# Expert biases spread by TensorE, gate columns stored apart, one expert's weights moved behind a store

## The reference, cut to what matters

```python
y = depthwise_causal_conv(x, cond)                 # called z in the kernel
logits = einsum('bsd,de->bse', y, Wr)
w, sel = top_k(logits, 2); w = softmax(w)
gate = einsum('bsk,bske->bse', w, one_hot(sel))
for e in range(8):
    out = out + gate[..., e:e+1] * (einsum('bsd,df->bsf', y, We[e]) + be[e])
return x + out
```

## Time and profile before

| | us |
|---|---|
| median of 3 runs (lowest, highest) | 823.74 (822.41, 827.26) |
| the profiled execution | 826.98 |
| its span in the profile | 824.9 |
| TensorE busy | 725.0 |
| VectorE, ScalarE, GpSimd busy | 532.0, 437.5, 503.9 |
| mean granted TensorE clock, share of full speed | 0.952 |

### The profile page before, as it was taken

How to read it: one execution, slowest core, us unless ns; L and a number is a source line. 1 busy time by engine, 2 the same in 40 slices (tenths; PEclk the granted TensorE clock), 3 DMA queues, 4 the chain that set the end, 5 groups by cost and what they waited for, 6 DMA issues and landing times.

```text
span 824.9 us, 13278 instructions
## 1 busy us (share of the span) xinstructions
PE 725.0 (88%) x3769; PEld 477.0 (58%) x3808; DVE 532.0 (64%) x765; ACT 437.5 (53%) x721; POOL 503.9 (61%) x760
## 2 busy tenths in 40 slices
PE   1753689999999999999999969995679999999995
PEld 0111235555555555565555559994558888888883
DVE  2466989898889888848876533576454445454542
ACT  2054457777778777847777511573443333434331
POOL 1036788787777777748773420003568888888773
PEclk9985889999999999989999988998799999999998
DMA  9986135566776766646667557698978989888983
GB/s 357 387 312 182 33 64 100 122 131 150 146 166 138 142 147 150 136 102 137 135 123 133 105 100 163 130 301 208 277 159 156 161 162 160 164 157 164 159 156 41
DMA packets 233113, 132.25 MB, mean 160 GB/s; under 512 B 182402, under 2 KB 198786, under 8 KB 231890
## 3 DMA queue, kind: packets, MB, share of 16 engines
q1 hardware_dynamic: 212866, 93.75, 46.8%
q0 software_dynamic: 15904, 35.48, 23.3%
q10 hardware_dynamic: 4272, 2.18, 1.3%
HBM read 74.44 MB, written 37.78 MB: 136 GB/s over the span
## 4 chain that ended last, share of the span: by engine, by line
PE 74%; DMA 10%; SPq 7%; DVE 3%; issue 2%; POOL 2%; ACT 1%; POOLq 0%; DVEq 0%; ACTq 0%
PE PS L1758 21%; PE PS L1615 12%; PE PS L1592 12%; PE PS L1604 12%; PE PS L1669 7%; PE PS L1636 3%; PE PS L1740 3%; DMA WRAW<-in_We 3%; SPq L429 3%; DMA WRT<-in_Wr 2%; PE PS L1645 2%; DMA z_scratch<-ZS 2%; PE PS L1627 2%; DMA QyT<-Qy 2%; SPq L515 1%
## 5 line engine op out<-in xcount | busy, mean ns | idle before, releaser
L1758 PE MATMUL PS<-W,ZH 128*128 x568 | 184.7, 406 | 7.1 <-DVE ZL L1498 7.0
L1592 PE MATMUL PS<-W,QyT 128*128 128x512 bf16 x499 | 126.0, 393 | 28.2 <-DMA QyT<-Qy 17.8
L869 POOL DMA_INDIRECT ZR<-z_scratch,IDG x71 | 78.9, 1112 | 94.6 <-DVE IDG L1466 60.6
L878 POOL DMA_INDIRECT out_x<-YS,IDS x71 | 112.7, 1587 | 39.3 <-issue 19.5
L1104 ACT ACTIVATE YS<-YS,SG 128x512 f32<-128x512 f32 x71 | 51.4, 724 | 138.5 <-DVE YS L1517 130.9
L1604 PE MATMUL PS<-W,QyT 128*128 128x512 bf16 x500 | 122.4, 384 | 0.6
L1758 PEld LDWEIGHTS PS<-W,ZH 128*128 128x128 f32 x568 | 103.1, 191 | 26.8 <-issue 8.4
L1615 PE MATMUL PS<-W,QT 128*128 128x512 bf16 x498 | 113.8, 379 | 0.7
L1498 DVE TENSOR_TENSOR ZL<-PS,ZH 128x512 fp32r<-128x512 f32 x71 | 49.1, 692 | 100.0 <-ACT ZH L1093 100.0
L1758 PE MATMUL PS<-W,ZL 128*128 x284 | 112.5, 396 | 0.0
L939 ACT ACTIVATE SG<-PS,sm 128x1024 f32<-128x1024 f32 x64 | 71.4, 1115 | 60.2 <-PE PS L1592 60.2
(11 more groups left out here) (249 smaller groups left out, 1110.9 us busy)
## 6 DMA issues: line engine op xcount, KB each, us to landing
X<-in_x SPq DMA_DIRECT2D x32, 256.0 KB, 10.0
out_x<-X SPq DMA_DIRECT2D x32, 256.0 KB, 2.5
WRAW<-in_We SPq DMA_DIRECT2D x32, 256.0 KB
ST<-out_x SPq DMA_DIRECT2D x28, 256.0 KB, 3.8
XR<-in_x SPq DMA_DIRECT2D x20, 256.0 KB, 3.6
stage<-in_w1T SPq DMA_DIRECT2D x4, 1024.0 KB, 8.0
stage<-in_w2T SPq DMA_DIRECT2D x4, 1024.0 KB
stage<-in_w3T SPq DMA_DIRECT2D x4, 1024.0 KB, 11.7
```

Of the source, the lines that this page charges most:

```text
L869: pool.indirect_dma_start(ZR[m % UZ][:, 0:ZW].bitcast(I32), None, z_d, bass.IndirectOffsetOnAxis(IDG[:, m:m + 1].bitcast(U32), 0)) \
L878: pool.indirect_dma_start(x1_d, bass.IndirectOffsetOnAxis(IDS[:, m:m + 1].bitcast(U32), 0), YS[m % UN][:], None, bounds_check=TOK - 1, oob ...
L1592: i = nc.tensor.matmul(GP[:, a, :], QyT[t][:, k, :], W12[:, k, o:o + CH], start=(k == 0), stop=(k == KD - 1))
L1758: x = nc.tensor.matmul(bank[i], zz[i % 2][:, k, :], W2[:, bass.ds(q, 1), part, k, :].rearrange("p o d -> p (o d)"), start=(k == 0 and n == ...
```

## The change

- `be` is loaded into partition 0 of `BEB` alone (16 KB). A product of a row of ones (`ONER`) with a row of `BEB` spreads it over the 128 partitions in PSUM (`bias`), and ScalarE copies it back to `BEB` (`copy_bias`). Experts 0 and 1 are done before slot 0, experts 2 to 7 in slot 1, in banks 6 and 7 by turns.
- The two gate columns have a store of their own for each half (`store_gates`), issued by SyncE: in half 0 after part 2, in half 1 before part 0. Part 2 no longer holds them.
- Expert 2's weights are loaded with those of experts 3 to 7, after all stores have landed.
- ScalarE's order becomes: `z_high(1)`, scale 0, `high(2)`; scale 1, six `copy_bias`, `z_high(2)`, `high(3)`, `high(4)`; and on as before.

```diff
+        def store_gates(queue, h):
+            queue.dma_start(bass.AP(z_d.tensor, h * BH * S * ZW + D, [[OB * ZW, P], [ZW, OB], [1, ZW - D]]),
+                            ZS[h][:, :, D:ZW].bitcast(I32)).then_inc(z_out[h], 16)
...
             for part in range(3):
                 sp.wait_ge(z_done, SPLIT[part + 1])
-                if part == 2:
-                    sp.wait_ge(gates_in, 1)
                 store_z(sp, 0, part)
-            sp.wait_ge(z_out[0], 48)
-            sp.dma_start(BEB[:].rearrange("p e d -> p (e d)"), bass.AP(be.tensor, 0, [[0, P], [1, E * D]])).then_inc(be_in, 16)
+            sp.wait_ge(gates_in, 1)
+            store_gates(sp, 0)
+            sp.wait_ge(z_out[0], 64)
+            sp.dma_start(BEB[0:1].rearrange("p e d -> p (e d)"), bass.AP(be.tensor, 0, [[E * D, 1], [1, E * D]])).then_inc(be_in, 16)
             load_expert(1)
             sp.wait_ge(conv_done, NG + 7)
             load_expert(0)
             sp.sem_inc(z_out[1], 1)
+            sp.wait_ge(gates_in, 2)
+            store_gates(sp, 1)
             sp.wait_ge(z_done, NG + SPLIT[1])
             store_z(sp, 1, 0)
-            sp.wait_ge(conv_done, NG + 11)
-            load_expert(2)
             sp.wait_ge(slots_done, 1)
...
             sp.wait_ge(first_done, 1)
-            sp.wait_ge(z_out[1], 49)
-            for e in range(3, E):
+            sp.wait_ge(z_out[1], 65)
+            for e in range(2, E):
                 load_expert(e)
...
-            act.wait_ge(gates_in, 2)
             act.wait_ge(z_done, 2 * NG)
             store_z(nc.scalar, 1, 2)
+            def copy_bias(e):
+                act.wait_ge(bias_done, e + 1)
+                nc.scalar.copy(BEB[:, e, :], bank[6 + e % 2]).then_inc(bias_read, 1)
+            copy_bias(0)
+            copy_bias(1)
             high(1)
...
                 if m + 1 < MT and m + 1 != LATE:
                     z_high(m + 1, (i + 1) % UN)
-                if m == 0:
-                    high(2)
                 act.wait_ge(bank_read, m + 1)
                 act.wait_ge(gate_done, m + 1)
                 nc.scalar.activation(YS[i][:], YS[i][:], ACT.Copy, scale=SG2[i][:]).then_inc(ys_done, 1)
                 if m + 1 == LATE:
+                    for e in range(2, E):
+                        copy_bias(e)
                     z_high(m + 1, (i + 1) % UN)
-                if m + 3 < E:
+                if m == 0:
+                    high(2)
+                if m == 1:
+                    high(3)
+                if 1 <= m < E - 3:
                     high(m + 3)
...
-                if m == 0:
-                    dve.wait_ge(be_in, 16)
+                if m < E:
+                    dve.wait_ge(bias_read, m + 1)
...
+            def bias(e):
+                if e == 0:
+                    pe.wait_ge(one_done, 1)
+                    pe.wait_ge(be_in, 16)
+                if e == 1:
+                    pe.wait_ge(slots_done, 3)
+                if e == 2:
+                    pe.wait_ge(first_done, 2)
+                if e >= 2:
+                    pe.wait_ge(bias_read, e - 1)
+                nc.tensor.matmul(bank[6 + e % 2], ONER[:], BEB[0:1, e, :], start=True, stop=True).then_inc(bias_done, 1)
             pe.wait_ge(slots_done, 1)
+            bias(0)
+            bias(1)
             turn_r(0, 0)
...
                 if m + 1 == LATE:
+                    for e in range(2, E):
+                        bias(e)
                     turn_r(m + 1, (i + 1) % UN)
```

More of the change, by code:

```diff
@@ L283, in adaln_ffn_moe @@
         a += 3 * NK
+        ONER = place("ONER", a, [1, P])
+        a += P
         assert a <= a_s + 8 * D + 5 * (D // 2) + 2 * D + FF // 2
@@ L344, in adaln_ffn_moe @@
         gate_done, bank_read, first_done = (sem(n) for n in ("gate_done", "bank_read", "first_done"))
+        one_done, bias_done, bias_read = sem("one_done"), sem("bias_done"), sem("bias_read")
         trz_done, zh_done, zl_done, exp_done, ys_done = (sem(n) for n in ("trz_done", "zh_done", "zl_done", "exp_done", "ys_done"))
@@ L357, in store_z @@
             first, end = (GI * NJ * SPLIT[part + i] for i in range(2))
-            if part + 2 == len(SPLIT):
-                end = ZW
             queue.dma_start(bass.AP(z_d.tensor, h * BH * S * ZW + first, [[OB * ZW, P], [ZW, OB], [1, end - first]]),
                             ZS[h][:, :, first:end].bitcast(I32)).then_inc(z_out[h], 16)
+        def store_gates(queue, h):
+            queue.dma_start(bass.AP(z_d.tensor, h * BH * S * ZW + D, [[OB * ZW, P], [ZW, OB], [1, ZW - D]]),
+                            ZS[h][:, :, D:ZW].bitcast(I32)).then_inc(z_out[h], 16)
         def piece_of(g):
@@ L627, in _ @@
             sp.sem_inc(z_out[1], 1)
+            sp.wait_ge(gates_in, 2)
+            store_gates(sp, 1)
             sp.wait_ge(z_done, NG + SPLIT[1])
             store_z(sp, 1, 0)
-            sp.wait_ge(conv_done, NG + 11)
-            load_expert(2)
             sp.wait_ge(slots_done, 1)
-            halves = [sp.value_load(FLAG[0:1, m:m + 1], min_val=1, max_val=49) for m in range(LATE)]
+            halves = [sp.value_load(FLAG[0:1, m:m + 1], min_val=1, max_val=65) for m in range(LATE)]
             for half in halves:
@@ L841, in _ @@
             pool.memset(ONB[:], 1.0).then_inc(route_p, 1)
+            pool.memset(ONER[:], 1.0).then_inc(one_done, 1)
             pool.memset(TRI[:], -1.0).then_inc(route_p, 1)
@@ L867, in gather @@
                 if m == LATE:
-                    pool.wait_ge(z_out[1], 49)
+                    pool.wait_ge(z_out[1], 65)
                 pool.indirect_dma_start(ZR[m % UZ][:, 0:ZW].bitcast(I32), None, z_d, bass.IndirectOffsetOnAxis(IDG[:, m:m + 1].bitcast(U32), 0)) \
@@ L1451, in _ @@
             v(nc.vector.tensor_tensor(HTOP[:, 0:UN], HTOP[:, 0:UN], IOSF[0:1, 1:UN + 1], ALU.is_lt))
-            v(nc.vector.tensor_scalar(FLAG[:], HTOP[:, 0:UN], 48.0, 1.0, ALU.mult, ALU.add))
+            v(nc.vector.tensor_scalar(FLAG[:], HTOP[:, 0:UN], 64.0, 1.0, ALU.mult, ALU.add))
             v(nc.vector.tensor_reduce(TEF[:], GE[:], AX.X, ALU.add))
@@ L1761, in slot @@
                 if m == 0:
+                    pe.wait_ge(bias_read, 1)
                     for j in range(UN + 1):
```

## The result

The changed kernel is slower by 0.9%: median 833.27 us of five runs (830.57 to 834.19) against 826.13 us of five runs of the kernel before; ratio 1.0091, 95% interval 1.0071 to 1.0111. It lies above the forecast (825.2) and above the end of its range (831.0). The forecast was made against a median of 823.74 for the kernel before; set against the kernel before it said 1.5 us more, and 7.1 us more were measured. The profiled execution took 834.19 us, 1.9 more than its span of 832.3, which is 7.4 above the span before.

The account below looks back on a forecast made before the run. Bound: waits for the last z store and expert weights up to slot 7, then TensorE. Store 4.7 us earlier, then 3.0 and 7.8 later, +6.1 at slot 2, mostly given back: 1.5 later, 825.2 us; range 820.5 to 831.0.

Parts of the forecast that it names:

- its twin: The same-sized z store of half 0, landing 7.6 us after issue; taken as the last store's time once its queue empties.
- 1 and 2, the queue ahead of the store: Before the last z store: removing bias megabytes (up to 7.4 us) and expert 2's load (3.7) empties the queue near 558.
- 3, the gate columns: Separate 8-byte-piece stores before half 1's other parts: 0.6 us delay for the last store, between 0 and 3.7.
- Rival B: The 8-byte stores hold half 1's z store, shifting everything after it by 3.7 us: 828.9; chance 0.10.
- 5, expert 2 behind the store: Expert 2's weights land at 575.4, 8.35 us after issue; conversion, low part and addition follow, slot 1's scaling to 581.7.
- 6, copies and products: After slot 1's scaling: products 4 to 6 at half clock, 7 at full; slot 2 at 590.7, 6.1 us later.
- At half clock for all 7.4: Bad end for the bias products before slot 2: all four at half clock, delay 7.4 us instead of 6.1.
- 7, what is given back: Slots 2 to 7: shorter slot 2 (4.5 us), weight waits gone (17.4 from slot 3); slot 7 only 1.5 us later.
- 8, GpSimd at cost 0: Scatters start later, scatter 5 at 613 to 617, but slack of 2.3 to 5.6 us covers it: cost 0.
- signs that it is too low: Scatter 5 starting after 618, or VectorE's addition waiting for out_x from slot 8 on.
- Rival A: GpSimd's gathers and scatters become the bound beyond a 4 us lag; slots 6.2 us later, 829.9; chance 0.15.
- the 834 of all bad ends: Sum's slow extreme, about 834 us: half clock, 3.7 for gate columns, 2.6 of weight waits; cut from the range.

Follow-up runs that it names:

- B alone: Kernel before with only the bias rows spread by products and copies, in the changed ScalarE order; ratio 0.9992 to the kernel before.
- E alone: Kernel before with only expert 2's weights loaded behind the stores and the changed ScalarE order, bias by DMA; ratio 1.0004 to the kernel before.
- experiment 2: Changed kernel with the gate columns stored with part 2 again, no store of their own; ratio 1.0072 to the kernel before.
- experiment 8: Changed kernel with gate columns joined and bias rows 4 to 7 made one each in slots 2 to 5; ratio 0.9994 to the kernel before.
- experiment 3: Changed kernel with the six bias copies moved from slot 1 into slot 0, ahead of expert 2's conversion; ratio 1.0042 to the kernel before.
- experiment 9: Changed kernel with 36 unused full-size products between bias products 3 and 4, to keep TensorE's clock; ratio 1.0079 to the kernel before.
- experiment 12: Changed kernel with expert 7's load moved into SyncE's slot loop, so scatters are released before it; ratio 1.0074 to the kernel before.
- experiment 11: Kernel before with the gate columns stored apart in half 0 only; ratio 1.0038 to the kernel before.
- experiment 7: Kernel before with bias by products, ScalarE's old order, rows 2 and 3 in slot 1, rows 4 to 7 one each in slots 2 to 5; 823.66 us, ratio 0.995.
- experiment 5: Kernel before with only the gate columns of both halves stored apart; ratio 1.0077 to the kernel before.

## Why the prediction was wrong

The line of events was the one forecast, and so was its sign; nearly each term in it came out too small. Two steps failed most. The last store was to take 8.2 us (7.6 by its twin, 0.6 for the gate columns) and took 10.23. And TensorE was to be back at full clock for the last product and for slot 2, but it ran at half clock through all four products, tile 2's transposes (which the sum had left out) and slot 2: 2.5 us more in parts 6 and 7. A third step, GpSimd's lag at no cost, failed by 1.0 us. In the order of the prediction's numbers:

- **1 and 2, the queue ahead of the store: right in kind, too good by 1.5 us.** B alone and E alone bring the landing from 12.9 to 10.0 and 10.4, both together to 9.1 (experiments 2 and 8), not to the twin's 7.6. That "the queue is empty near 558" did not hold: the DMA share was 1.25 and 1.20 from 556 to 560. Gathers 0 and 1 run beside this store and not beside its twin; whether they are the 1.5 us was not tried apart.
- **3, the gate columns, priced too low.** The prediction took 0.6 us with 3.7 as the end, by STL's reads. Measured on the landing: 1.1 (9.1 to 10.2) in the changed kernel, where the queue is short; 12.2, 12.9 and 13.0 in experiments 3, 9 and 12, whose queue is the same, thus up to 3.9; 4.6 over B alone, 5.5 over E alone, 6.2 over the kernel before. The fuller the queue, the dearer, and in half 0 too (experiment 11). The Trainium skill, "DMA: Bandwidth & Descriptors", Specifications, says that below 512 B a transfer is done by read-modify-write and misses line rate; the runs agree that small writes are dear, and the prediction was wrong to put a read's row above it. Rival B names this cost. Its 3.7 is inside what was seen with this queue, but in the changed kernel's own trace the columns cost 1.1, and joining them again gave back nothing that the ratios resolve (experiment 2): the loss against the forecast is not mainly rival B.
- **5, expert 2 behind the store.** Right, and the store's delay passes on: landed 578.34 (forecast 575.4), 9.6 us behind its first issue instead of 8.35. ScalarE started at once instead of 0.6 later. The scaling of slot 1 ended at 583.94, forecast 581.7; 1.65 of that is the store.
- **6, copies and products.** The size failed at the clock. "At half clock for all 7.4" stood in the text as the bad end, and it was the case; the last product was not yet at full. The sum also left out tile 2's transposes, which stand behind the last product on TensorE and took 1.06 us of the chain at half clock. From scaling to slot 2 this made 10.2 us instead of 9.0. Experiments 7 and 8 show that the line itself, not its clock alone, is the loss: with two copies in it, slot 2 follows the scaling by 2.3 us in experiment 7.
- **7, what is given back.** The pace from slot 3 to 7 was right (17.1, forecast 17.4, no wait for weights). But slot 2, forecast at 4.5 us by ScalarE's conversions, took 5.50 at half clock and set slot 3 by itself (5.8 after slot 2). The kernel before already had its slot 2 at 0.50, so this was there to be read.
- **8, GpSimd at cost 0.** Wrong by 1.0 us. Scatter 5 was forecast at 613 to 617 and started at 621.97; against slot 7 it is 4.5 us later than before. The gathers in between remained long (3.00 and three times 2.34 or 2.35; the first is in the rows below). Both of the prediction's signs that it is too low came: scatter 5 after 618, and additions that wait for `out_x` from slot 8 on. Rival A, which decides "from a lag of 4 us", holds in small: 1.0 us, where it puts 829.9, 4.7 above the forecast.

GpSimd's timeline in the changed kernel:

```profile
573.92 0.95 POOL L876 DMA_INDIRECT ZR<-z_scratch,IDG  x1 [0.30 <-issue]
598.64 1.63 POOL L885 DMA_INDIRECT out_x<-YS,IDS  x1 [23.77 <-SPq L660]
600.57 3.00 POOL L876 DMA_INDIRECT ZR<-z_scratch,IDG  x1 [0.30 <-issue]
...
618.78 1.59 POOL L885 DMA_INDIRECT out_x<-YS,IDS  x1 [1.59 <-ACT YS L1116]
620.67 0.99 POOL L876 DMA_INDIRECT ZR<-z_scratch,IDG  x1 [0.30 <-issue]
621.97 1.59 POOL L885 DMA_INDIRECT out_x<-YS,IDS  x1 [0.30 <-issue]
```

The sum in the profile: the store 1.65 late, expert 2 and its conversion 0.6, from the scaling to slot 2 1.25, slot 2's clock 1.25, slots 3 to 7 0.3 less: 4.5 at slot 7 (617.07 against 612.6). With GpSimd's 1.0 and the 0.4 ahead of the last scatter it is 5.9, from the forecast span of 826.4 to 832.3. A forecast made of many small terms, each taken near its good end, misses by their sum: the range of its own mechanism reached only 829, the whole range 831.0, and the 834 of all bad ends was cut off as unlikely.

Open: why the landing with small pieces varies from 10.2 to 13.0 between kernels with the same queue, where without pieces it came out as 9.1 twice (in experiments 3, 9 and 12 the bias load went out 22.0 to 22.1 us ahead of the last store, in the changed kernel 22.9, without pieces 24.9 to 25.3: a hint, not a proof); how a fuller queue makes the pieces dearer; and why slot 2 ran at half clock in experiment 9 after products of full size.

## What to carry to other kernels

Work moved onto a wait hides only as long as nothing later is queued behind it on the same engine: take each engine's order and lay the moved work, at the worst clock, behind the latest arrival. Put small products and copies one to a slot instead of in a block; here that turned a loss of 0.7% into nothing (experiment 8), and with expert 2 left early into a gain of 0.5% (experiment 7). And keep narrow columns in the row of a wider store: in the full queue two stores of 16 KB made the last store 6.2 us later, where taking expert 2's megabyte out of that queue gained 2.5.

## What the runs showed of the hardware

- **Small writes to DRAM.** A store of 2,048 pieces of 8 bytes (16 KB) delays what is queued with it by 1 to 4 us in a short queue and by up to 6.2 in a full one (two such stores), and the next issue of the same engine is held for 4.2 to 8.8 us instead of 0.55. The store itself lands in 8.6 us (changed kernel) to 10.9 (experiment 5), STL's reads, 2,048 pieces of 32 bytes, in 4.0. Behind the pieces the DMA engines moved 57 GB/s at a share of 0.79, where they moved 258 before.
- **One-row products and the clock.** They keep TensorE busy and the granted clock falls to 0.50 all the same (experiment 3). A 512-column float32 product of one row takes 1.8 us there (7.19 for four), and 0.94 at full clock (3.77 for four).
- **A lag of GpSimd stays.** A gather and a scatter take it 3.19 us, a slot takes TensorE as long, so what it is behind before slot 7 is hardly caught up: the scatter of slot 7 starts 8.1 us after that slot's addition instead of 3.6, and the scatter of slot 60 still 6.9 instead of 3.6. The slots waited up to 0.9 us at a time for it, and the 1.0 us that they came later by is the part that is gone.
